# Splitting the key stores to DRAM by parts instead of by head halves, in a transformer block with routed experts

## The reference, cut to what matters

```python
x = x + L0_xattn(norm(x), ctx)   # cross attention, self attention, FFN (gelu), each with add and norm
x = x + L0_ffn(norm(x))          # mixture of experts: top 2 of 8, 7 real experts with 256 slots each
x = x + L1_xattn(norm(x), ctx)   # second cross attention, 16 heads of 16
x = x + L1_ffn(norm(x))          # mixture of depths: half of the tokens go through an FFN
```

## Time and profile before

| | us |
|---|---|
| median of 3 runs | 921.56 |
| lowest, highest | 911.32, 923.29 |
| the profiled execution, its own time | 923.29 |
| its span, first to last instruction | 921.6 |
| around the span | 1.7 |

### The profile page before, as it was taken

The page is one execution under the profiler, slowest core; times in us unless marked ns, Lnnn a source line. Parts: engine busy times, 40 slices in busy tenths (PEclk is TensorE's granted clock), DMA queues, the critical chain, the costliest instruction groups (busy, mean ns, idle before and its releaser), DMA issues.

```text
span 921.6 us, 17014 instructions
## 1 busy us (share of the span) xinstructions
PE 782.0 (85%) x6622; PEld 635.2 (69%) x6622; DVE 564.4 (61%) x1166; ACT 434.7 (47%) x728; POOL 383.5 (42%) x372
## 2 busy tenths in 40 slices
PE   4578999999999878999997799992547888779897
PEld 4456777777777547999897688882434566548896
DVE  5357887888888653898873111111656798755432
ACT  3135767677777566664633311120114566664232
POOL 6465573443465363746444130004554355242200
PEclk9679999999999999999997899996656899999999
DMA  8966776657764601201073776552473675500011
GB/s 185 167 118 107 122 123 101 97 102 133 110 112 94 82 2 48 69 24 42 17 263 93 216 264 229 158 114 62 79 112 54 103 119 97 83 2 1 23 36 35
DMA packets 60548, 92.15 MB, mean 100 GB/s; under 512 B 8978, under 2 KB 35601, under 8 KB 59652
## 3 DMA queue, kind: packets, MB, share of 16 engines
q1 hardware_dynamic: 56498, 83.68, 44.0%
q0 software_dynamic: 3072, 6.04, 2.9%
q10 hardware_dynamic: 898, 1.34, 0.9%
HBM read 45.13 MB, written 16.40 MB: 67 GB/s over the span
## 4 chain that ended last, share of the span: by engine, by line
PE 67%; DVE 13%; DMA 7%; issue 5%; POOL 3%; ACT 3%; SPq 2%; another core or an unknown queue 1%; POOLq 0%; DVEq 0%; ACTq 0%
PE ps L701 8%; PE ps L195 7%; PE ps L766 7%; PE ps L197 6%; PE ps L196 6%; DVE nmax L1459 6%; PE ps L861 6%; PE ps L875 5%; PE ps L723 5%; PE ps L219 4%; PE ps L914 3%; PE ps L924 3%; PE ps L740 2%; ACT prob L1048 1%; POOL gat L1322 1%
## 5 line engine op out<-in xcount | busy, mean ns | idle before, releaser
L1459 DVE TENSOR_REDUCE nmax<-ps 128x4 f32<-128x1024 f32 x192 | 234.7, 1225 | 98.6 <-PE ps L701 96.6
L1048 ACT ACTIVATE prob<-ps 128x1024 f32<-128x1024 f32 x192 | 196.5, 1023 | 81.7 <-PE ps L723 79.1
L1233 POOL TENSOR_TENSOR rstd<-var,half 128x2 f32<-128x2 f32 x56 | 43.7, 780 | 279.1 <-DVE var L1398 202.0
L701 PE MATMUL ps<-kst,qst 50*128 50x256 f32 (+1 forms) x768 | 101.9, 347 | 45.2 <-DVE nmax L1459 31.3
L701 PEld LDWEIGHTS ps<-kst,qst 50*128 50x128 f32 (+1 forms) x768 | 61.8, 199 | 87.9 <-DVE nmax L1459 47.1
L766 PE MATMUL ps<-prob,vext 128*32 128x256 f32 x1536 | 108.0, 401 | 0.6 <-ACT oext L1061 0.6
L723 PE MATMUL ps<-qst,kst 51*128 51x256 f32 (+1 forms) x768 | 83.0, 295 | 20.4 <-DMA qst<-m_hi 10.5
L723 PEld LDWEIGHTS ps<-qst,kst 51*128 51x128 f32 (+1 forms) x768 | 62.1, 195 | 27.1 <-ACT prob L1048 13.4
L1604 DVE COPY vext<-ps 128x512 f32<-128x512 f32 x7 | 4.8, 692 | 100.8 <-PE ps L875 50.9
L766 PEld LDWEIGHTS ps<-prob,vext 128*32 128x32 f32 x1536 | 41.4, 112 | 33.1 <-issue 5.3
L1061 ACT ACTIVATE oext<-ps 128x256 f32<-128x256 f32 x96 | 37.0, 386 | 43.7 <-PE ps L740 24.8
(11 more groups left out here) (299 smaller groups left out, 2060.8 us busy)
## 6 DMA issues: line engine op xcount, KB each, us to landing
qst<-q_parts SPq DMA_DIRECT2D x138, 128.0 KB, 3.9
kst<-k_parts SPq DMA_DIRECT2D x93, 128.0 KB, 5.5
e_in<-in_ein SPq DMA_DIRECT2D x5, 1024.0 KB, 5.1
e_out<-in_eout SPq DMA_DIRECT2D x5, 1024.0 KB, 8.0
k_park<-kpart SPq DMA_DIRECT2D x16, 256.0 KB, 4.4
kst<-k_park SPq DMA_DIRECT2D x16, 256.0 KB, 6.1
ctx_raw<-in_ctxT SPq DMA_DIRECT2D x8, 256.0 KB, 6.5
v_park<-vext SPq DMA_DIRECT2D x8, 256.0 KB, 4.1
```

The lines of the kernel that those rows point to most:

```text
L701: last = pe.matmul(score_pair(n, p)[:, 512 * s + S * t:512 * s + S * (t + 1)], qst[j][a:b, p, t * P:(t + 1) * P], kst[j][a:b, p, :], start ...
L1048: act.activation(probs[p % 4][:].rearrange("p i t s -> p (i t s)"), T_PS, ACT.Exp).then_inc(sm["exp_done"], 1)
L1459: dve.tensor_reduce(nmax[n % 2][:, :, :, p].rearrange("p t s -> p s t"), score_pair(n, p).rearrange("p (s t k) -> p s t k", s=2, t=TB), AX ...
```

## The change

The two key stores of a batch are cut by part c instead of by partition half s. Each takes all 128 partitions of one part, 128 rows of 2 KB, 256 KB. The same bytes go to the same addresses, with the same two issues and the same semaphore increments.

```diff
                     sp.wait_ge(sm["k_split"], n + 1)
-                    for s in range(2):
-                        sp.dma_start(k_park[b, s].rearrange("c p x -> p c x"), park_k(b)[64 * s:64 * s + 64].rearrange("p c t x -> p c (t x)").bitcast(F32)).then_inc(sm[f"park{b % 4}"], 16)
+                    for c in range(2):
+                        sp.dma_start(k_park[b, :, c], park_k(b)[:, c].bitcast(F32)).then_inc(sm[f"park{b % 4}"], 16)
                     sp.wait_ge(sm["park_s"], b + 1)
```

## The result

The changed kernel takes 961.2 us in the median of four runs (959.5 to 963.4), the kernel before 922.4 in its four (911.3 to 924.7): a ratio of 1.045, 95% interval 1.036 to 1.054. The profiled execution took 964.5 against 923.3. The forecast was 966, range 950 to 1000.

A forecast was written before the change was run, and what follows sets the result against it. TensorE's in-order work was taken as the bound, with the stores hidden; stores queued on two engines make expert 1 41.0 us late, plus 2.0 for restart: 43 us on the profiled 923.3, so 966 us, range 950 to 1000.

The forecast's parts named there:

- What bounds: TensorE's in-order work, busy 782.0 of 921.6 us; key stores hidden, TensorE idle 5.28 us ahead of expert 0's tokens.
- Parts 1 and 2: Key stores: unchanged issues cost nothing extra; the 128-partition source up to twice as fast, 0.7 us not 1.4, worth nothing.
- Part 3: Key stores' DRAM side: outermost dimension from 64 to 2 puts each store on two engines, 5.4 us a store.
- reading of a 16 KB copy: Line 552's copy, outermost 2 on one side, moves 33 to 49 GB/s alone: read as about two engines at work.
- The sum: Stores queue on the same two engines: expert 0 30 us late, expert 1 41.0, plus 2.0 for restart: 43 us.
- the term of the batch: One batch's work on the two engines: 2 x 5.42 us for keys and 0.68 for values, 11.5 us.
- A wait put at nothing: Reuse wait of batches 4 and 5 for earlier stores: met in time, only batches 6 and 7 held.
- The restart: Expert 1 on TensorE restarts after an idle time at a lower granted clock: 2.0 us.
- the signs: Line 475's stores landing up to some 50 us after issue, long stretches near 50 GB/s, TensorE waiting for both token loads.
- Rival 1: Key stores spread over 16 engines after all, wider source halves a store; 0 to 1 us freed, 922 us; chance 0.07.
- rival 3: Key stores on two engines at the 64-partition stores' rate, 11.7 GB/s an engine; about 1059 us; chance 0.07.
- Rival 2: Key stores on two engines each, but other ones each time, so no line; some 3 us, 926 us; chance 0.06.

The follow-up runs named there:

- one-block kernel: Changed kernel with each full-width key store sent to one contiguous 256 KB block in DRAM instead of two blocks; 918.0 us, ratio 1.000 to the kernel before.

## Why the prediction was right

- **What bounds.** Right: stores hidden, the tokens of expert 0 the one exposed place. The one-block kernel shows that the form of the stores is free as long as 16 engines carry them.
- **Parts 1 and 2.** The wide source: no gain, as forecast. The issue cost was put at nothing and that was wrong in kind: the second key store and the value store of a batch took some 5 us each to issue. As far as the sum tells it cost nothing of its own, since the data stood in the same line.
- **Part 3, two engines at 24.2 GB/s each.** Right in count and rate, 49 GB/s for the two. The forecast's reading of a 16 KB copy carried over to 256 KB stores; its mean of 17.8 GB/s an engine did not. That the two are the same for every store was taken without a row; the token rows 224 to 32 now show it.
- **The sum.** A batch was put at 11.5 us; the waits that end at 510.36 and 521.29 give 10.9. The first store came 2.9 us earlier in this execution, so I compare from the first store on. Expert 0's tokens were taken up 71.3 us after it against 43.3 before, 28.0 late (forecast 29.7), expert 1's 99.3 against 61.1, 38.2 late (forecast 41.0). The 2.8 us too much are for the most part the term of the batch.
- **A wait put at nothing.** The keys of batch 5 were forecast to be in time; they waited 5.13 us. It cost nothing at the end, for batch 7 waited for the same line later.
- **The restart.** Put at 2.0 us, measured 10.22 - 7.17 = 3.05 in fc1 of expert 1, at a granted clock of 0.70, and 0.5 more in the transposes of its tokens (1.11 against 0.60), 3.6 in all.
- **A term not in the sum.** In the last layer the stretch 862.4 to 962.8 has the same waits as 825.6 to 921.6 before but lasts 4.4 us more, all of it busy time of TensorE; its first 25 us have a mean granted clock of 0.77, against 1.00 before. Nothing in the records ties this to the stores: in the profiles of the eight other kernels every 25 us of the last 100 have 0.93 or more. 38.2 + 3.6 - 2.9 + 4.4 = 43.3, against 41.2 in the span; the 2.1 between lie in the stages between, and I did not trace them.
- **What was luck.** The profiled execution took 964.5 us and the forecast was 966, but 4.4 us of it are this unforeseen term. By medians the loss is 961.2 - 922.4 = 38.8 us against the 43 of the sum, a tenth less.
- **Where the reading of the signs was wrong.** I expected stores that land up to 50 us after their issue. SP's queue holds them back instead, so that batch 3's last store, issued at 507.11, had ended by 521.29, 14 us later, 5.08 of them the issue itself, and the tokens of expert 0 landed 9.8 us after their issue. So some 9 us of line stand in front of the engines, and the rest of the lateness is in the issues ahead, which I had named only as a possibility.
- **The rivals.** Rival 1 (16 engines) and rival 3 (the rate of the earlier trace rows) are refuted by the 49 GB/s. Rival 2 (other engines each time) is refuted by the token rows, of which exactly two sixteenths were late, and by the rate, which would reach 98 at times.

The two profiles of the last layer, by stretch (us, busy of PE, PEld, DVE, ACT, POOL, PEclk, DMA share, GB/s), after and then before:

```profile
862.00:887.00 25.00, 23.88 (x178) 18.42 (x171) 10.64 (x43) 11.82 (x24) 5.37 (x7) 0.77 0.00 1
```

```profile
825.60:850.00 24.40, 23.28 (x210) 19.49 (x207) 13.80 (x57) 12.34 (x26) 5.21 (x6) 1.00 0.00 1
```

## What to carry to other kernels

Before a DMA's access pattern is rewritten, look at the outermost dimension of both its sides: the number of engines that carry it depends on it, and 2 there made a hidden 256 KB store take 5.4 us on two engines and put all later transfers of its queue behind it, as far as they need these two engines. A small DMA with the same outermost size told the rate beforehand here. For background traffic add up the engine time for each queue against the time in which it is issued; the loss begins where the line reaches a load that TensorE waits for, and so depends on which stores are slow and on what stands behind them.

## What was not expected of the hardware

- Issues on SyncE get long behind loaded engines: some 5 us for the second key store and for the value store of a batch beside two loaded engines, 0.6 us where 16 engines share the rows.
- A transfer that is spread over 16 engines is late by its share on the loaded ones alone: 224 rows of the tokens at once, the other 32 some 5 us after them.
- A transfer given from another queue passes such a line: 5.9 us for the tokens from ScalarE's queue beside two loaded engines. It is not free of it, though: the same load took 3.0 us in the one-block kernel, and the scatter from GpSimd completed after 7.5 us beside four loaded engines instead of 2.1, though after 3.5 beside two. What held it there stays open.
